# Pairs of scan products added on GpSimd, a later and an earlier start of four kinds of work, and new step sizes for the planner of a four-block layer kernel

## The reference

```python
delta = softplus(dt_full + b_dt)
def step(state, inp):
    dA = exp(dlt[..., None] * A_g)
    state = dA * state + (dlt * u)[..., None] * Bs
    y = einsum('bgdn,bgn->bgd', state, Cs)      # sum over the 16 states
    return state, y
y = (y + x * D_param) * silu(z); return y @ W_out.T
```

## Time and profile before

| | |
|---|---|
| median of 3 runs (1944.04 to 1947.22) | 1946.99 us |
| the profiled execution's own time | 1944.15 us |
| its span, first to last instruction | 1942.4 us |
| up to the first scan | 242.6 us |
| scan of sequence 0, to the first scan of 1 | 193.8 us |
| sequences 1 to 5 together | 1053.1 us |
| sequence 6; sequence 7 | 203.4; 157.7 us |
| after the last scan | 91.8 us |
| busy PE, DVE, ACT, POOL | 83%, 78%, 62%, 52% |

### The profile page before, as it was taken

The page is one execution under the profiler, slowest core; times in us unless marked ns, Lnnn a source line. Parts: engine busy times, 40 slices in busy tenths (PEclk is TensorE's granted clock), DMA queues, the critical chain, the costliest instruction groups (busy, mean ns, idle before and its releaser), DMA issues. The chain is left out here.

```text
span 1942.4 us, 22619 instructions
## 1 busy us (share of the span) xinstructions
PE 1609.7 (83%) x5868; PEld 716.1 (37%) x5948; DVE 1521.5 (78%) x2808; ACT 1198.9 (62%) x2035; POOL 1000.3 (52%) x772
## 2 busy tenths in 40 slices
PE   2266488878997899979998899889997999789856
PEld 0113123323452346333552345234633354235224
DVE  5384599979998898969897998889986878586920
ACT  4347765677669575857577766957685536743421
POOL 0100645594449544764459444964477445864720
PEclk9987689879998899979998999989997899799988
DMA  4010022322223222322232222322232223232300
GB/s 117 2 48 22 25 85 95 111 80 79 92 92 110 73 85 77 121 77 75 87 107 81 87 88 85 115 73 90 71 121 77 82 92 119 75 111 93 123 1 11
DMA packets 94601, 157.95 MB, mean 81 GB/s; under 512 B 10940, under 2 KB 23660, under 8 KB 94468
## 3 DMA queue, kind: packets, MB, share of 16 engines
q1 hardware_dynamic: 94468, 156.43, 24.4%
HBM read 143.83 MB, written 12.58 MB: 81 GB/s over the span
## 5 line engine op out<-in xcount | busy, mean ns | idle before, releaser
L1401 POOL TENSOR_TENSOR prod<-state,c_all 128x512 f32<-128x512 f32 x512 | 653.0, 1280 | 550.5 <-DVE state L1378 436.1
L1378 DVE TENSOR_TENSOR_SCAN state<-decay,ps_b 128x512 f32<-128x512 f32 x512 | 621.8, 1214 | 53.3 <-ACT decay L1121 30.2
L924 PE MATMUL ps_y<-prod,idf 128*128 128x512 f32 x1024 | 606.2, 685 | 18.2 <-DVE u L1391 9.7
L1121 ACT ACTIVATE decay<-delta,a_neg 128x512 f32<-128x512 f32 x512 | 362.7, 721 | 222.6 <-DVE state L1378 221.9
L1385 DVE TENSOR_TENSOR ps_b<-du,ps_b 128x512 f32<-128x512 f32 x512 | 349.1, 682 | 87.2 <-PE ps_b L917 86.4
L917 PE MATMUL ps_b<-b_rows,sel_b 48*128 48x512 bf16 x512 | 207.3, 408 | 74.5 <-DVE state L1378 72.7
L924 PEld LDWEIGHTS ps_y<-prod,idf 128*128 128x128 f32 x1024 | 174.3, 203 | 165.1 <-issue 107.3
L917 PEld LDWEIGHTS ps_b<-b_rows,sel_b 48*128 48x128 bf16 x512 | 47.1, 93 | 376.5 <-DVE state L1378 234.0
L793 PE MATMUL ps_x<-xT,w 128*128 128x512 bf16 (+1 forms) x386 | 130.4, 417 | 30.7 <-DVE arena_l L1284 12.0
L896 PE MATMUL ps_x<-arena_b,fcT 128*128 128x512 f32 x256 | 125.4, 613 | 6.2 <-ACT arena_b L1103 5.5
L709 PE MATMUL ps_x<-hT,win 128*128 128x512 bf16 (+1 forms) x449 | 114.5, 388 | 13.3 <-DVE arena_b L1350 6.8
(11 more groups left out here) (236 smaller groups left out, 2411.1 us busy)
## 6 DMA issues: line engine op xcount, KB each, us to landing
c_all<-c_rows SPq DMA_DIRECT2D x512, 256.0 KB
c_rows<-arena_l SPq DMA_DIRECT2D x32, 256.0 KB
out<-arena_b SPq DMA_DIRECT2D x8, 512.0 KB
x_in<-in_base SPq DMA_DIRECT2D x8, 256.0 KB
c_all<-in_winT SPq DMA_DIRECT2D x1, 1280.0 KB, 7.1
arena_b<-in_w_fc SPq DMA_DIRECT2D x1, 1024.0 KB, 5.8
arena_b<-in_w_proj SPq DMA_DIRECT2D x1, 1024.0 KB, 4.7
w<-in_w1T SPq DMA_DIRECT2D x1, 792.0 KB, 5.8
```

Source lines behind the costliest of these rows:

```text
L924: nc.tensor.matmul(ps_y[:], idf[:], prod[:, n % NP, :], start=(n % NST == 0), stop=(n % NST == NST - 1)).then_inc(reduced, 1)
L1121: nc.scalar.activation(decay[:, n % NDA, :], delta[:, slot(s, ct), :], ACT.Exp, scale=a_neg[:, ct, st:st + 1]).then_inc(decayed, 1)
L1378: nc.vector.tensor_tensor_scan(state[:, n % NS, :], decay[:, n % NDA, :], ps_b[:, n % NDB, :], 0.0, ALU.mult, ALU.add).then_inc(scanned, 1)
L1401: nc.gpsimd.tensor_tensor(prod[:, n % NP, :], state[:, n % NS, :], c_all[:, n % NC, :], ALU.mult).then_inc(multiplied, 1)
```

## The change

Six things change at once. (1) Of every four scan steps, the products of the first two (`n % 4` is 0 or 1) are added on POOL into the first one's buffer, and PE sums the pair once. (2) The softplus steps of the four channel tiles stand nine rounds apart rather than one or two, in the order 0, 3, 1, 2. (3) `quant` moves beside the first sequence's `early`, and both weights are loaded at the start into buffers of their own. (4) Ahead of the first scan only `late` of 0 up to `du` of tile 0 must be done; what is left of it and of `early` of 1 is woven into the first iteration, with a table of urgencies of its own (`FIRST`). (5) `back` of the last sequence rotates over four PSUM banks. (6) Eight kinds of steps are halved (`proj`, `gram`, `fc`, `wout`, `x4`, `apply`, `add`, `gate_root`), the output is stored in two halves, and the planner has new durations, by part where these differ, knows ACT's table loads and waits between parts, and has new urgencies.

```diff
+D_ORDER = (0, CT - 1) + tuple(range(1, CT - 1))
+D_AT = tuple(D_ORDER.index(i) for i in range(CT))
...
-    d0 = (14, 15, 17, 18)
     for i in range(CT):
-        k = d0[i]
+        k = 15 + 9 * D_AT[i]
...
+FIRST_HALF = {"proj": "proj_a", "gram": "gram_a", "fc": "fc_a", "wout": "wout_a", "x4": "x4_a", "apply": "apply_a", "add": "add_a",
+              "gate_root": "gate_root_a"}
...
-SCAN_BUSY = {"decay": 62, "spread": 33, "drive": 60, "scan": 114, "product": 125, "sum": 87, "taken": 66, "load": 6}
+SCAN_BUSY = {"decay": 62, "spread": 33, "drive": 60, "scan": 114, "product": 123, "pair": 122, "sum": 96, "taken": 66, "load": 6}
+TABLE_LOAD = 128
...
+def in_pair(n):
+    return n % 4 < 2
...
-URGENT = {"late": (0.32, 0.21, 0.17, 1.42, 0.34, 0.61, 0.01, 0.02),
+URGENT = {"late": (0.27, 0.05, 0.22, 1.66, 0.06, 0.03, 0.0001, 0.0001),
...
+FIRST = {"late": (42.9, 24.5, 7.37, 44.6, 3.04, 338, 3.77, 11),
...
+        def back_bank(s, i):
+            return (XB, 0, 1, 2)[i % 4] if is_seq(s, NBATCH - 1) else XB
...
+            elif name in ("fc_a", "fc"):
+                if name == "fc_a":
...
+                    if back_bank(s, 1) == XB:
+                        free = ("f_turned", 1) if i == 0 else ("relu", i - 1)
+                    else:
+                        free = ("f_turned", 1) if i < 4 else ("relu", i - 4)
+                    eng.wait_ge(back["A"], bk(s, "A", free))
...
                 for n in sums_at(j):
...
+                    two = in_pair(n)
+                    if n % NST == two:
+                        wait(eng, y_taken, s.count(PER, n - two))
+                    if two:
+                        eng.wait_ge(paired, s.count(PER, pairs_to(n)))
+                    else:
+                        eng.wait_ge(multiplied, s.count(PER, n + 1))
+                    nc.tensor.matmul(ps_y[:], idf[:], prod[:, (n - two) % NP, :], start=(n % NST == two),
+                                     stop=(n % NST == NST - 1)).then_inc(reduced, 1 + two)
...
                 nc.gpsimd.tensor_tensor(prod[:, n % NP, :], state[:, n % NS, :], c_all[:, n % NC, :],
                                         ALU.mult).then_inc(multiplied, 1)
+                if in_pair(n) and n % 2 == 1:
+                    eng.wait_ge(multiplied, s.count(PER, n + 1))
+                    nc.gpsimd.tensor_tensor(prod[:, (n - 1) % NP, :], prod[:, (n - 1) % NP, :], prod[:, n % NP, :],
+                                            ALU.add).then_inc(paired, PAIR_TILES)
...
-            together(e, eng, fns, tagged("late", Seq(0), LATE), tagged("early", Seq(1), EARLY), tagged("quant", None, QUANT))
-            iteration(e, eng, fns, Seq(0), first=True)
+            alone(e, eng, fns, tagged("early", Seq(0), EARLY), extra, tagged("quant", None, QUANT), QUANT_FROM)
+            late0 = Chain(tagged("late", Seq(0), LATE), (1000,) * 8)
+            early1 = Chain(tagged("early", Seq(1), EARLY), (1,) * 8)
+            order, _ = weave([late0, early1], range(0), -1, (), (late0, place_of(LATE, ("du", 0)) + 1))
+            run_order(e, eng, fns, Seq(0), order)
+            iteration(e, eng, fns, Seq(0), (late0, early1))
```

More of the change, by code:

```diff
@@ L364, in head @@
     def head(self, e):
-        if self.at >= len(self.rounds):
+        if self.at >= len(self.rounds) or not all(chain.over() for chain in self.after):
             return None
@@ L387, in weave @@
     port = {"V": 0, "G": 0}
+    table = ("exp", "tanh")
     done, order = {}, {e: [] for e in "PAVGS"}
     def ready_at(deps):
[L392 removed]
+        deps = [d for d in ((kind, now + by, step) for kind, by, step in deps) if d in own]
         return None if any(d not in done for d in deps) else max([0] + [done[d] + HANDOVER for d in deps])
     for _ in range(sum(len(v) for v in scan.values()) + sum(sum(chain.left) for chain in chains)):
+        if until is not None and until[0].over(until[1]):
+            break
         best = None
```

379 lines of the change are left out of this document (198 added, 181 removed).

## The result

The changed kernel takes 2051.25 us (median of 4 runs, 2050.21 to 2053.26) against 1947.11 us for the kernel before beside it: a ratio of 1.054, 95% interval 1.052 to 1.0554. It is slower by 104 us where 97 us of gain were forecast. The profiled execution has a span of 2048.6 us, 106.2 more than before.

A forecast was written before the change was run, and what follows sets the result against it. The bound was taken to walk from engine to engine, PE first with DVE close behind. Against 1944 us the terms -34 + 8 - 50 + 0 - 7 - 11 = -94 gave 1850 us, range 1780 to 1905.

The forecast's parts named there:

- Part 1: Pairs in the scan: PE loses 17 us a sequence, 189 to about 172; POOL gains 20.5; old order alone gains 1 or 2.
- Part 2: New order in sequences 1 to 5: 10 us gained a sequence, 50 for five.
- eight counted pieces: Largest engine's work in each eighth of a sequence's scan steps, summed: 207.0 us in the old order, 199.4 changed.
- The port: DVE instructions in the loop, lengthened beside POOL's: 2 us a sequence at most, inside the 10 us booked for the new order.
- Part 3: The start: less work ahead of the first scan, -34 us (bounds -50 and -15), first scan at about 208 us.
- Part 4: Sequence 0: it gets the work that left the start, +8 us.
- Part 5: Sequences 6 and 7: 0 booked for sequence 6 and -7 us for 7.
- Part 6: The end after the last scan: four banks, halved steps and earlier output, -11 us.
- C: Rival: slower, POOL's queue sets the pace in the loop and the additions come on top whole; +112, 2056 us; chance 0.04.
- D: Rival: pairs summed so late that `ps_y` delays `u`; +96 us, ending at 1946, no change; chance 0.02.

The follow-up runs named there:

- relief-alone run: The kernel before in its own order, with the even product of each pair left unsummed and nothing added on GpSimd: 1944.31 us, ratio 0.9985.
- pair's run: The kernel before in its own order, with only the pair's addition on GpSimd, written over the first product, and 384 sums for 512: 1985.11 us, 1.0178.
- pairs' order without pairs: The changed kernel's own order, planned for pairs, but TensorE sums both products singly and GpSimd adds nothing: 2037.38 us, 1.0442.
- unpaired run: The changed kernel without pairs, 512 single sums and no addition on GpSimd, order planned anew: 1987.93 us, 1.0186.
- short additions: The changed kernel in the same order, with the pair's addition on GpSimd covering 4 of 512 columns: 2030.38 us, 1.0404.
- before's order in the loop: The changed kernel without pairs, softplus groups close, sequences 1 to 7 ordered by the planner of the kernel before: 1953.73 us, 1.0029.

## Why the prediction was wrong

**What bounds.** The reading that the bound walks from engine to engine held, and it was the warning: what is taken from one engine shows only where that engine has a piece to itself. In the relief-alone run two pieces of eight shrank by more than 1 us.

**Part 1.** "In the old order the pair alone is worth 1 or 2 us a sequence": it costs 7.8 (total +34). PE's busy time did not fall to 172 but to 184 in the pair's run, and not at all after, 193. I took 17 us of sums off at full clock and left the rest of PE's time as it was; the clock of sequence 4 was 0.92 for 0.97 and the rest grew. And the step from "PE-bound piece" to "gives up two sums" had nothing on the buffer of the first product, which PE now frees one sum later. The forecast of POOL's busy time, 145 us a sequence and 1165 in all, was right (146.4 and 1168.3): the load was right, the queue behind it missing. By the prediction's own rows DVE leads POOL by 2.0 us in the seventh piece, so two additions there should have cost 0.5 us and not 2.6; with that the booked gain would have been 3 us, still of the wrong sign.

**Part 2.** "-10 us a sequence" is the term that failed most: +18. The eight counted pieces, 199.4 in sum, measure 228.1 in sequence 4: 37.7, 28.6, 23.1, 24.1, 33.1, 23.2, 19.8 and 38.5. The third, fourth and seventh are within 1.1 us. The first is 8.5 short and the last, with the seam, 12.9. The last is the fourth softplus group: a chain through PE, ACT and POOL in which no engine has much to do. A count of work per engine cannot see it. The first is DVE, busy for 37.3 of 37.7 us, and for 34.6 of 35.9 in the pairs' order without pairs: the count took before's durations for its instructions. Added up one by one in the trace they take 42.0 us there; the same instructions at before's mean durations would take 36.8, so 5 of the 8.5 us are stretched instructions. The order alone, without any pair executed, makes the loop 226.6 us, 16 over before; this the fit of the count to before's 208.6 had hidden, since in before's order the busiest engines of the pieces add up to 205.4 us, 3 short of the sequence. In the changed kernel's sequence 4 the same sum is 214.4, and 14 us are covered by no one engine.

**The port, "2 us a sequence at most".** DVE went from 184 to 193. Two groups of DVE, before and then after:

```profile
L1369 DVE TENSOR_TENSOR rm<-rs_o,rm 128x4 f32<-128x4 f32 x8 | 1.1, 143 | 1.1 <-POOL rs_o L683 1.1
...
L1149 DVE TENSOR_SCALAR arena_e<-x_in,mb_x 128x256 bf16<-128x256 bf16 x32 | 12.1, 438 | 0.4 <-ACT vb_x L967 0.4
```

```profile
L1447 DVE TENSOR_TENSOR rm<-rs_o,rm 128x4 f32<-128x4 f32 x8 | 7.2, 895 | 1.1 <-POOL rs_o L743 1.1
...
L1225 DVE TENSOR_SCALAR arena_e<-x_in,mb_x 128x256 bf16<-128x256 bf16 x32 | 20.5, 701 | 0.4 <-ACT vb_x L1042 0.4
```

Total DVE: 1521.5 before, 1544.9 unpaired, 1555.1 in the pairs' order without pairs, 1563.8 with short additions, 1578.7 after. More than half of the 57 us, 34, come with the order and no addition at all; with before's order in the loop, halves and all, the total is 1522.4. The traces show that it is the neighbours. DVE's scaling of 128x256 bf16 (the second group's form, 192 in all) takes 276 ns in the mean where it runs clear of every POOL instruction, before and after; the 62 that overlap one took 454 ns before, and the 69 after take 724. In the pairs' order without pairs it is 59 at 684 ns, and of the 115 instructions on 128x4 fp32, 0.15 us when clear, 30 overlap one and take 0.89 us, where before's were 10 at 0.75. These two forms make some 30 of the 34 us. I had priced POOL's share of time and not which instruction stands beside which. The Trainium skill ("SBUF — State Buffer", section "SBUF: two separate sides") names a lock on a shared port pair. The trace agrees in this: the scan and the drive, with one input in PSUM, stayed at 1216 and 680 ns, and the first group, with two SBUF inputs, was stretched. Whether the second group runs in one of the modes that the lock covers no run shows.

**Part 3** came out right in sum: first scan at 210.1 for 208. Its terms were not taken apart; with the groups close the first scan is at 226.4. **Part 4**, +8, was +41.5: the seam of sequence 0 is 46.3 us long, POOL busy for 29.5 of it and PE's clock 0.59. What left the start came back, and more; start and sequence 0 together gained nothing (445.4 for 436.4), and in the unpaired run 6 us. **Part 5**, 0 for sequence 6: +21.9. I had named the pile of the last experts in eight steps, 62 us of PE, and booked 0 because PE's total falls; the piece takes 70.7 us, PE busy for 70.4 of it, and the same piece takes 70.3 with the pairs' order alone and 46.8 in the unpaired run. The count itself had +3.0 for sequence 6 and -5.8 for 7, so booking 0 and -7 went 4 us beyond it. Sequence 7 gave 3.2 of 7. **Part 6**, -11, gave -10.5; its single terms were not tested.

**Rivals.** C, "slower, 2056", is 5 us from the result, but by luck: its condition, POOL over 95% busy in more than half of a sequence, holds in one piece of eight, and taking away the additions' length won 21 us, not 164. Its sign, over 100 us of idle time before scans, did not come either (68.3 us). No rival had the order itself as the loss. D's condition, sums too late for `u`, is only a small part: DVE's waits for `ps_y` are 57 us for 36 before, nearly all in the seams.

**In short.** Two steps failed. One is Part 2: a count of work per engine was taken for the length of a piece. In its place the runs showed chains across engines at the seams (spread groups, +31 us by themselves), stretched DVE instructions, and an order for pairs that costs 49 us before any pair is executed. The other is Part 1: PE's relief was booked at full clock and with no price for the held buffer. In its place it gave at most 14 us of 134 where nothing was added and the buffer was free at once. How the rest of that relief divides between the clock and DVE stays open, and so does why the new planner's order is dear for pairs beyond the pieces named.

## What to carry to other kernels

Where the busiest engine changes every eight steps, first leave the work out of one engine (no sum, no replacement) and time that: it bounds the idea in one run. Here it gives 3 us, and 14 with the buffer freed at once, and that would have been known before any addition was written. A count of work per engine did not price this order, because a chain crossed engines; look at the last chain to finish before each seam separately. And when two buffers become one, try writing the result over the one that is free latest anyway: here that was worth 13 us.

## What the runs showed of the hardware

- Relief of TensorE came with a lower clock. With a quarter of the fp32 sums gone and nothing in their place, the granted clock of sequence 4 fell from 0.97 to 0.92 and over the run the half of a sum took 731 ns instead of 685.
- The same work at the same clock can be granted a different clock next. With sums left out in steps 8 to 39, the unchanged end took 96.3 us for 91.8. In the 30 us ahead of it TensorE is equally busy and at 1.00 in both; then come the end's first 10 us, 0.68 in that run and 1.00 in before. Why it falls in the one and not in the other no run shows. So some 5 us of a difference between two kernels can come from a stretch that neither of them changed. First that run, then before:

```profile
1819.60:1849.60 30.00, 25.68 (x68) 8.47 (x69) 28.91 (x34) 10.21 (x16) 23.78 (x19) 1.00 0.36 122
1849.60:1860.00 10.40, 7.30 (x17) 4.61 (x16) 0.77 (x2) 0.00 (x0) 2.52 (x2) 0.68 0.01 2
```

```profile
1820.60:1850.60 30.00, 25.69 (x68) 8.48 (x69) 28.92 (x34) 10.23 (x16) 23.80 (x19) 1.00 0.36 123
1850.60:1861.00 10.40, 6.63 (x25) 4.18 (x24) 0.79 (x2) 0.59 (x1) 2.52 (x2) 1.00 0.00 0
```

- A DVE instruction on 128x4 elements, 0.14 us by itself, took 1.23 us beside a GpSimd instruction. Scans, with one input in PSUM, took 1211 ns clear of every GpSimd instruction and 1218 beside one in the kernel after. Between before's order and the one for pairs, with no addition in either, DVE's busy time differs by 34 us.
